# State-space block of a two-layer decoder: the sum over states as accumulating DMAs into SBUF, and the rows of B and C read back from DRAM for all partitions

## The reference, cut to what matters

```
xz = x @ W_in;  x_in, z = split(xz)
xc = silu(conv(x_in) @ pw_kernel + conv_bias)
x_dbl = xc @ W_x                       # 16 columns of delta, 8 of B, 8 of C
delta = softplus(x_dbl[:16] @ W_dt + b_dt)
h[t] = exp(delta * A[n]) * h[t-1] + delta * B[t, n] * xc    # for each state n
y[t] = sum over n of C[t, n] * h[t, n]
y = (y + xc * D) * silu(z)
return y @ W_out
```

## Time and profile before

| What | Value |
|---|---|
| Time, median of 3 runs | 2914.62 us (2907.15 to 2915.93) |
| Span of the profiled execution, first to last instruction | 2910.6 us |
| The block's groups, from DVE's first scan to the next stage's first instruction | 104.67 to 744.45 us |
| Busy in the stretch 350 to 450 us: PE, DVE, ACT, POOL | 92.09, 93.22, 67.69, 4.39 us of 100 |
| Transfers in that stretch | none |

### The profile page before, as it was taken

One profiled execution on the slowest core, in us unless ns is written; L12 is line 12 of the kernel. 1 busy time (PEld: TensorE's weight loads), 2 busy tenths in 40 slices (PEclk: granted clock), 3 DMA queues, 4 the chain that ended last, 5 costly groups with the idle time before them and its releaser, 6 DMA issues. The chain is left out here.

```text
span 2910.6 us, 60882 instructions
## 1 busy us (share of the span) xinstructions
PE 2622.9 (90%) x21142; PEld 1775.5 (61%) x21143; DVE 1977.7 (68%) x4470; ACT 1613.8 (55%) x3119; POOL 439.5 (15%) x450
## 2 busy tenths in 40 slices
PE   6799999996799999999887799999999899969993
PEld 3344444443466677676676467777777645558993
DVE  2699999999577777777667467777777555661223
ACT  2666666763266666666545456666666333305553
POOL 0000000000300000000022211111110032324551
PEclk9999999998899999999887889999999889969997
DMA  4000000000100000000000100000000120002225
GB/s 118 0 1 0 0 0 0 0 1 0 37 22 21 21 16 21 20 17 21 1 15 1 41 23 21 21 21 21 21 21 11 48 90 20 14 18 66 70 70 174
DMA packets 57927, 80.55 MB, mean 28 GB/s; under 512 B 8880, under 2 KB 47058, under 8 KB 57490
## 3 DMA queue, kind: packets, MB, share of 16 engines
q1 hardware_dynamic: 51778, 62.69, 7.5%
q0 software_dynamic: 6048, 16.52, 1.8%
HBM read 63.59 MB, written 15.60 MB: 27 GB/s over the span
## 5 line engine op out<-in xcount | busy, mean ns | idle before, releaser
L1309 DVE CUSTOM_DVE_ANT_0 xa_h_scores<-xa_h_score_bank,xa_h_added 112x375 f32<-112x375 f32 x1024 | 517.7, 544 | 147.7 <-PE xa_h_score_bank L1244 133.2
L1403 ACT ACTIVATE xa_h_probs<-xa_h_scores,xa_h_negmax 112x375 f32<-112x375 f32 x1024 | 561.3, 600 | 0.8 <-DVE xa_h_negmax L1316 0.6
L1256 PEld LDWEIGHTS xa_h_turn_bank<-keep_ident,xa_h_probs 112*125 112x125 f32 x3072 | 396.2, 189 | 91.7 <-DVE xa_h_probs_t L1323 23.1
L1256 PE MATMUL xa_h_turn_bank<-keep_ident,xa_h_probs 112*125 112x112 f32 x3072 | 436.0, 278 | 9.3 <-DVE xa_h_probs_t L1323 9.0
L1323 DVE COPY xa_h_probs_t<-xa_h_turn_bank 125x448 f32<-125x448 f32 x512 | 318.8, 623 | 149.1 <-PE xa_h_turn_bank L1256 135.6
L1409 ACT ACTIVATE xa_h_probs_t<-xa_h_turn_bank 125x448 f32<-125x448 f32 x256 | 138.6, 541 | 301.4 <-PE xa_h_turn_bank L1256 301.2
L663 DVE TENSOR_TENSOR_SCAN mb_state<-mb_decay,mb_drive 128x1792 f32<-128x1792 f32 x64 | 249.4, 3896 | 0.9 <-ACT mb_decay L594 0.2
L1244 PE MATMUL xa_h_score_bank<-xa_h_keys,xa_h_queries 32*112 32x375 f32 x2048 | 231.7, 522 | 10.8 <-DVE xa_h_row_max L1309 10.2
L1269 PEld LDWEIGHTS xa_h_sums_bank<-xa_h_probs_t,xa_h_values 125*32 125x32 f32 x6144 | 141.1, 110 | 154.1 <-DVE xa_h_probs_t L1323 149.0
L455 PE MATMUL mb_y_bank<-mb_read_out,keep_ident 128*128 128x448 f32 x448 | 199.2, 592 | 33.4 <-DVE mb_read_out L679 23.7
L1269 PE MATMUL xa_h_sums_bank<-xa_h_probs_t,xa_h_values 125*32 125x112 f32 x6144 | 201.5, 264 | 14.4 <-issue 6.0
(11 more groups left out here) (366 smaller groups left out, 4055.4 us busy)
## 6 DMA issues: line engine op xcount, KB each, us to landing
xa_context<-in_ctx_t SPq DMA_DIRECT2D x64, 375.0 KB, 3.1
lm_w<-in_m_w SPq DMA_DIRECT2D x16, 512.0 KB, 9.9
lm_e_wide<-lm_result_rows SPq DMA_DIRECT2D x8, 896.0 KB, 9.5
keep_x<-in_x SPq DMA_DIRECT2D x4, 896.0 KB, 16.6
lm_latent_rows<-lm_rows SPq DMA_DIRECT2D x8, 448.0 KB, 3.2
out_x<-keep_x SPq DMA_DIRECT2D x8, 448.0 KB, 6.5
xa_mask_raw<-in_key_mask SPq DMA_DIRECT2D x1, 1312.5 KB
mb_f_pw<-in_pw SPq DMA_DIRECT2D x1, 1024.0 KB
```

What stands on the lines that cost most here:

```text
L1256: last = pe.transpose(turn_bank[(par + kc) % 2][0:KP, g * S:(g + 1) * S], probs[par][:, g, kc * KP:(kc + 1) * KP], keep.ident[0:S, 0:S])
L1309: dve.tensor_tensor_reduce(scores[par][:, g, :], score_bank[g][0:S, 0:SK], added[s][:, :], 1.0, -BIG, ALU.add, ALU.max, row_max[par][:, g: ...
L1403: act.activation(probs[par][:, g, :], scores[par][:, g, :], ACT.Exp, bias=negmax[s][:, G * c + g:G * c + g + 1]).then_inc(probs_ready, 1)
```

## The change

The rows: ACT keeps `low` as before, SP stores its 16 rows of B and C to a DRAM tensor `low_rows` (28,672 bytes per group), and then SP loads, for each state, two rows of 448 numbers into all 128 partitions with a partition stride of zero (458,752 bytes written per state, in 256 pieces of 1,792 bytes), into one of four slots. A slot is loaded again once the read-out that used it is done. The split into bf16 parts, the matmuls of `spread`, the copies of `keep_rows` and the table `own_row` with its load and its cast are gone.

The sum: `y` lies in SBUF, in two buffers for groups in turn. ACT writes xc * D into it (`skip`, four activations of 128x448), and POOL issues for each state one DMA that adds `read_out` to `y` in flight (`accum_op`), 917,504 bytes each, 64 in all. Each waits until the one before it has landed. `add_pair`, `add_state`, the `skip` matmuls and the `y_bank` banks are gone. `finish` is now one multiplication of 128x1792 in place of four of 128x448, and stands after the read-out of n = 2 of the following group; `gates` gets two buffers for that. The loop over groups goes in pairs.

```diff
-        y_bank = [psum(f"y_bank{n}", [128, 512]) for n in range(IC)]
+        y = sb("y", [128, 2, IC, T])
-        rows = sb("rows", [128, 2, 2, T])
+        low, rows = sb("low", [4 * LOW, T]), sb("rows", [128, ROW_SLOTS, 2, T])
+        low_rows = nc.dram_tensor(name + "low_rows", (GROUPS, 2, N, T), F32).ap()
...
+            def store_low(g):
+                sp.wait_ge(low_read, g + 1)
+                sp.sem_inc(store_started, 1)
+                sp.dma_start(low_rows[bass.ds(g, 1)].rearrange("o k n t -> (o k n) t"), low[R:LOW, :]).then_inc(low_stored, 16)
+
+            def load_rows(g, n):
+
+                if n == 0:
+                    sp.wait_ge(low_stored, 16 * (g + 1))
+                reuse(sp, read_out_ready, N * g + n - ROW_SLOTS + 1)
+                sp.sem_inc(load_started, 1)
+                sp.dma_start(rows[:, n % ROW_SLOTS, :, :],
+                             low_rows[bass.ds(g, 1), :, n, :].broadcast_to([128, 2, T])).then_inc(rows_in[n % ROW_SLOTS], 16)
+
+            def group(g, k, at, final=False):
+                for n in range(N):
+                    load_rows(g, n)
+                if not final:
+                    store_low(g + 1)
...
+            def add_state(g, k, n):
+
+                pool.wait_ge(read_out_ready, N * g + n + 1)
+                if n == 0:
+                    pool.wait_ge(skipped, g + 1)
+                reuse(pool, summed, 16 * (N * g + n))
+                pool.sem_inc(add_started, 1)
+                pool.dma_start(flat(y[:, k, :, :]), flat(read_out[:, n % 2, :, :]), accum_op=ALU.add).then_inc(summed, 16)
...
-            def spread(g, n):
-                for k in range(2):
-                    reuse(pe, row_read[k], use_of_row(g, k, n))
-                    pe.matmul(row_bank[k][:, 0:T], own_row[:, k * N + n, :], low_parts[:, :], start=True, stop=True).then_inc(row_done[k], 1)
...
-                for c in range(IC):
-                    last = pe.matmul(y_bank[c][:, 0:T], keep.ident[:, :], read_out[:, n % 2, c, :], start=False, stop=n == N - 1)
-                last.then_inc(summed, 1)
...
-                    if n + 2 < N:
-                        spread(g, n + 2)
-                    if n != FIRST:
-                        add_state(g, n)
...
+            def skip(g, k):
+
+                for c in range(IC):
+                    last = act.activation(y[:, k, c, :], inner[:, c, :], ACT.Copy, scale=skip_w[:, c:c + 1])
+                last.then_inc(skipped, 1)
...
-                    if n + 1 < N:
-                        keep_rows(g, n + 1)
                     if n == 0:
-                        read_gates(g)
+                        read_gates(g, k)
+                        skip(g, k)
...
             def make_drive(g, n):
-                dve.wait_ge(row_read[0], use_of_row(g, 0, n) + 1)
+                dve.wait_ge(rows_in[n % ROW_SLOTS], loads_of_rows(g, n))
...
             def make_read_out(g, n):
...
+                reuse(dve, summed, 16 * (N * g + n - 1))
                 dve.wait_ge(state_ready, N * g + n + 1)
...
-            def finish(g):
-                dve.wait_ge(summed, PUSHES * (g + 1))
+            def finish(g, k):
+                dve.wait_ge(summed, 16 * N * (g + 1))
...
-                for c in range(IC):
-                    last = dve.tensor_tensor(gated_y[:, c, :], y_bank[c][:, 0:T], gates[:, c, :], ALU.mult)
-                last.then_inc(gated, 1)
+                dve.tensor_tensor(flat(y[:, k, :, :]), flat(y[:, k, :, :]), flat(gates[:, k, :, :]), ALU.mult).then_inc(gated, 1)
```

More of the change, by code:

```diff
@@ L337, in used, with loads_of_rows @@
             return sum(v % 2 == u % 2 for v in earlier + here[:here.index(u)])
[L339 to L345, removed]
-        def all_groups(eng, group):
[L349 to L353, removed]
+        def loads_of_rows(g, n):
+            return 16 * (N // ROW_SLOTS * g + n // ROW_SLOTS + 1)
+        def all_groups(eng, group):
+            group(0, 0, 0)
+            group(1, 1, 1)
+            with eng.Fori(1, GROUPS // 2 - 1) as i:
+                for k in range(2):
+                    group(2 * i + k, k, None)
+            group(GROUPS - 2, 0, GROUPS - 2)
+            group(GROUPS - 1, 1, GROUPS - 1, final=True)
         def flat(a):
@@ L462, in project_out @@
                 bank = front(g, u)
-                for k in range(2):
-                    b = 2 * half + k
+                for r in range(2):
+                    b = 2 * half + r
                     for c in range(IC):
-                        last = pe.matmul(bank[0:S, k * D:(k + 1) * D], gated_y[:, c, b * S:(b + 1) * S], w_out[:, c, :],
+                        last = pe.matmul(bank[0:S, r * D:(r + 1) * D], y[:, k, c, b * S:(b + 1) * S], w_out[:, c, :],
                                          start=c == 0, stop=c == IC - 1)
@@ L479, in group @@
                     if n == 0:
-                        gate(g, (0, 1))
-                        skip(g)
-                        gate(g, (2, 3))
+                        gate(g, range(IC))
                         if not final:
@@ L489, in group @@
                             low_rank(g)
-                        project_out(g, 0) if not first else pass_over(OUT_A)
+                        project_out(g, 1 - k, 0) if not first else pass_over(OUT_A)
                     if n == 6 and not final:
@@ L647, in make_delta @@
                 dve.wait_ge(log_ready, g + 1)
-                dve.tensor_tensor(flat(delta[:, :, :]), flat(above[:, :, :]), flat(soft[:, :, :]), ALU.add).then_inc(delta_ready, 1)
+                dve.tensor_tensor(flat(delta[:, :, :]), flat(delta[:, :, :]), flat(soft[:, :, :]), ALU.add).then_inc(delta_ready, 1)
                 dve.wait_ge(delta_ready, g + 1)
@@ L717, in group @@
                     make_read_out(g, n)
-                    if n == SECOND:
-                        add_pair(g)
+                    if n == 2 and not first:
+                        finish(g - 1, 1 - k)
                 if not final:
```

155 lines of the change are left out of this document (44 added, 111 removed).

## The result

The changed kernel takes 2842.31 us (median of 4 runs, 2840.61 to 2844.52), the one before 2915.27 in the same session (2907.15 to 2917.58): a ratio of 0.9755 [0.9743, 0.9768], 73.0 us. The rival "hidden throughout" (2850) is the case that came.

The account below looks back on a forecast made before the run. DVE and PE were nearly full, the gain hanging on DVE's chain. Pushes at P = 9.0 exceed the hidden 8.8, so 64 chained pushes rule: 2294.3 + 64 x 9.0 = 2870 us against 2914.6; 8-in-10 range 2848 to 3062.

Parts of the forecast that it names:

- hidden throughout: Rival: each push takes P under 8.8 us, so DVE's work hides all adding transfers; 2850 us, chance 0.33.
- DVE's own period, 70.3 us: DVE's time per group after the change without waiting for pushes: 68.4 + 1.95, 9.0 less than 79.3.
- Preamble -3.5, last group -0.4, tail +2.2: Around the groups: set-up and casts save 3.5 us, last group 0.4; gating behind the last read-out starts 2.2 later.
- P = 9.0: Time from a read-out's end, or the push before, to this push's landing: 9.0 us, giving 2870 us.
- two passes of 5.7 us: Data time of an adding push: source and old sum both read, 2.86 us per pass at 321 GB/s.
- The rows' share: Charge in P for row loads overlapping a push by about 1 us on the same engines; half charged.
- the limit: Largest P at which pushes stay hidden behind DVE's group of 70.3 us: 8.8 us.
- The period as the larger of 70.3 and 8P: A group takes DVE's 70.3 us or its eight chained pushes, 8P, whichever is larger.
- The formula 2294.3 + 64P: Kernel time beyond P = 8.8, with the block a chain of 64 pushes; equals the present time at P = 9.7.
- Rows not late: Next group's first rows, loaded behind a store waiting for `low`, land in time; rival of late rows under 2 in 100.
- PE at the lower clock: Rival: PE at 1.2 GHz needs 88 us per group, up to 2987 us; charged nothing, chance 3 in 100.
- The two prices by rule: Skill pages for a push: add at half rate for reading two sources; plain transfer 4.1 us, doubled data 6.2.

Follow-up runs that it names:

- the plain copy: Changed kernel with POOL's pushes copying the read-out into `y` without adding, so `y` holds the last state alone; 2837.77 us, ratio 0.9748.
- the sum alone: Kernel before with only the sum over states by adding transfers, rows still spread by PE and copied by ACT; 2888.95 us, ratio 0.9938.
- halves: Changed kernel with each push as two chained adding transfers of half the size; 2948.67 us, ratio 1.0127.
- the parts: Two kernels, each the kernel before with one part of the change: only rows by transfers, 2893.04 us; only the sum by transfers, 2888.95 us.
- run without them: Kernel with only the sum by transfers, its two POOL subtractions for the rows removed (B and C about three times too large); 2869.14 us, ratio 0.9851.
- the rows alone: Kernel before with only the rows of B and C by store and loads, sum over states still on PE with the pair addition; 2893.04 us, ratio 0.9932.

## Why the prediction missed, step by step

- **DVE's own period, 70.3 us: right.** The six middle groups take (590.56 - 168.75) / 6 = 70.30. They took 79.6 before; the first took 77.4 and now 66.9. Over the seven that is 66.5 us saved where the sum had 63.
- **Preamble -3.5, last group -0.4, tail +2.2: right to a microsecond.** First scan at 101.90, 2.8 earlier; last group 0.5 shorter; from the last read-out's start to the next stage 26.0 in place of 23.6, +2.4. With the groups 67.4, the 67.3 seen.
- **P = 9.0: the term that failed.** The prediction put it as 0.3 + 2.5 fixed, two passes of 5.7 us and 0.5 for the loads of the rows. The fixed part was right (2.6 measured against 2.8). Two passes of 2.86 us are refuted: the data take 4.2 us, and the plain copy is only 1.3 us shorter. That is 1.5 us too much for the data, the larger error. The rows' share was 0.4 too small: the 43 back-to-back gaps of the changed kernel run from 6.84 to 11.05 with a median of 7.76, while with no row loads (the sum alone) 10 gaps have a median of 6.86. Together P is 7.8 in place of 9.0. With P under the limit the forecast falls to its own 2850; that is 20 of the 28 us missed. Of the other 8, 3 lie in the groups and 5 in which executions make the median; the low end of 2848 left room for neither.
- **The period as the larger of 70.3 and 8P: wrong, and without effect here.** The chain pauses at each group's start, and six pushes must land before read-out 7, which DVE by itself starts at 60.5. The limit is 9.7 + 6P = 60.5 + 0.6, P = 8.6 in place of 8.8. The formula 2294.3 + 64P gives 2870 at 9.0; by the measured formula a group would be 9 + 9.7 + 54 = 72.7, the time 2850 + 7 x 2.4 = 2867, an estimate. The prediction's two formulas also don't meet at the limit: at P = 8.8 one gives 2850 and the other 2857. Above the limit a tenth of a microsecond costs, by the measured formula, 7 x 6 tenths and 8 in the last group, 50, not 64: a slower kernel was possible (halves: 2949), but the way up to the range's upper end, 3062 at P = 12, is less steep than the prediction supposed. So it is luck that this step did no harm: with P at 7.8 both limits are kept.
- **Rows not late: right.** No wait at L608; the rows land in 4.1 us against 3.2 assumed.
- **PE at the lower clock: there, and hidden.** PE's group of 52.9 us, not 44, at a granted 0.84, and DVE waited for the softplus 0.7 us from 170 to 660. The charge of nothing held: PE has 17 us per group in which it is not busy.
- **Where 73 come from when the parts give 41.** The medians make this look larger than it is. By the block's end the parts give 22.3 and 29.6 us, 51.9 of the whole's 67.3, and 14.3 of the 15.4 that are missing go when POOL's subtractions go (run without them): 22.3 + 43.9 = 66.2. So what looked like two parts helping each other is nearly all a wait that the second part alone brings with it, POOL's subtractions behind the pushes; the medians of both parts also hold some 6 us behind the block. What holds the kernel with the rows alone at 77.5 us a group is argued from its trace, not shown. Its waits read as one loop: DVE's `keep_x` (405.03) frees a bank for PE's gates, PE works in order through convolution and sums to the matmuls for delta (387.75 in the group before), ACT's softplus follows, then DVE's delta (396.77), and `keep_x` again. The sum on PE lies in that loop; that the loop alone sets the period was not tried by taking work from it.
- **The two prices by rule.** The Trainium skill (Collectives: The Full Stack, The bandwidth ceiling) has reduce-scatter at half the rate of all-gather, because its add reads two sources. The trace does not agree for this transfer: the addition makes 5.6 us into 6.9. The Trainium skill's estimate for a plain transfer (DMA: Bandwidth & Descriptors, Anatomy of one DMA, SWDGE path) was 4.1 us; 5.6 was measured in the median, 5.0 for two with little beside them. With its data doubled that estimate was 6.2 us, also hidden, as it came.

## What to carry to other kernels

Price a transfer that no row shows from its fixed part and its passes apart, then ask how many of them must fit between which two instructions: the first one's start and the buffer that is wanted back set the room, not the count per period. A queue that pauses once per group has slack at the pause, and chained work put there is free. When the parts of a change give less than the whole, compare them at the place that was changed before looking for a reason, and look for a wait that only the part alone has: here nearly all of the gap between 41 and 73 us was POOL's subtractions and time behind the block, where nothing was edited.

## What the runs showed of the hardware that was not expected

- An adding transfer of 917,504 bytes between SBUF tiles, issued by POOL, is 6.85 us from issue to issue undisturbed, half of it 4.74: by these two sizes 2.6 fixed and 217 GB/s. POOL's issue takes 0.86 us for an adding and 0.54 for a plain one.
- With loads of 448 KB in small pieces beside the pushes, the time from one push's issue to the next's was longer by 0.9 us in the median (7.76 against 6.86 without them), and at most 11.05 us against 8.31.
- DVE is not slowed by 159 to 164 GB/s of transfers on its tiles: scan 3.88, read-out 2.02, as before.
- POOL's subtraction of 64x448 took 1.97 us in the mean before, and with pushes in its queue 1.3 to 2.0 in four groups and 8.1 to 8.6 in three. What makes it so stays open; spans on POOL are rough, but DVE waited 4.7 us behind the long ones.
